# Layer 1's weights scaled in place with their low halves made by GpSimd, and four buffers for the first two units' probabilities

## The chip, the cores and the metric

The kernel runs on one core of a Trainium2 chip. The metric is the device time of one execution in microseconds (us); lower is better. TensorE (PE in the rows), VectorE (DVE), ScalarE (ACT), GpSimd (POOL) and the DMA queue of SyncE (SP, or SPq) work in parallel. Each runs its own list of instructions in order, and they wait for one another on semaphores only.

## The reference, cut to what matters

Two layers of masked attention over 128 graphs of 128 nodes, width 384, six heads of 64. Each layer is the same, with weights of its own:

```
h = max(layernorm(x), 0)                       # x: 128 x 128 x 384
q, k, v = h @ Wq + bq, h @ Wk + bk, h @ Wv + bv
probs = softmax(q k^T / 8 + (0 where adj else -9e15))
x = x + (probs @ v) @ Wf + bf
```

## The kernel before

A **unit** `t` is four graphs in one layer; there are 64 units (32 groups of graphs times two layers), and (t, i) is graph i of unit t. Units 0 to 3 belong to layer 0, unit 4 is the first one of layer 1, then the layers alternate. The work is a software pipeline written out by hand: a hand-written opening part, then `slot(t)` for t = 1 to 61, then a hand-written end (`last_units`). Every engine has a `slot(t)` of its own, and each goes through four quarters i = 0 to 3. In slot t TensorE forms the scores of unit t, the q, k and v projections of unit t + 1 (q and k in six chunks of 128 columns, two PSUM banks in turn), and the context products and output projections of graphs four to eight quarters back.

A float32 product is made as three float16 products of high and low halves (`three`, L665 to L667). So each weight needs a high half `w_hi` and a low half `w_lo`, both of the weight times a power of two, `w_scale`. Layer 0's are made in the opening part. Layer 1's are made in the quarters of slot 1, one weight per quarter in the order v, q, k, f: ScalarE writes `w_hi` (`weights_hi`, L915), VectorE writes `w_lo = w_raw * w_scale - w_hi` (`weights_lo`, L1207), each 128 x 1152. The first reader of layer 1's weights is the projection of unit 4, in slot 3.

The softmax chain of one graph: TensorE `score` (L779), VectorE `mask_and_min` (L1289), ScalarE `exp` (L986), VectorE `invert_sums`, GpSimd `scale_probs` (L540), VectorE `probs_turn` (L1230, a transpose in 32 x 32 blocks). Then SyncE's queue stores the blocks in DRAM (`keep_probs`, L360) and brings them back in turned order with four DMAs (`bring_probs`, L367), to `p_moved[i % 2]`. For units 0 and 1, TensorE multiplies `p_moved` with v in float32 (`apply_probs`, L759); from unit 2 on (`halved`), ScalarE casts the high half to `p_half` (`p_hi`, L961), GpSimd makes the low half (`p_lo`, L552), and the product has three float16 terms. h goes the same way over DRAM (`keep_h`, `bring_h`), and then `h_hi` (L940) and `h_lo` (L547) split it.

`p_half` is two tiles of 128 x 3 x 768 float16. Until unit 2 they hold no probabilities; layer 0's Wq and Wk are loaded into them at the start. There are two `p_moved` tiles, so the return of graph (t, i) waits until the graph two before it has been multiplied: `ctx_summed` counts the `apply_probs` done. For units 0 and 1 in the odd quarters SyncE's queue issues `bring_h` ahead of `bring_probs` (`late`).

Other names the steps touch: `ctx_hi` (L977) and `ctx_lo` (L1263) split a context product; `qk_hi_out` (L969) and `qk_lo_out` (L1269) take a chunk out of its PSUM bank, and the chunk two further on waits for that; `v_out` (L948) and `v_lo` (L1258) do so for v; `relu` (L926) waits for GpSimd's `norm` (L522 to L527), which waits for VectorE's `statistics`. TensorE's `project_v(t, i)` in the even quarters waits for `ctx_lo` of graph i of unit t - 2 (`ct_set`), `score(t, 0)` waits for the last `qk_lo_out` of unit t, and `apply_probs` of an odd graph i of unit t waits for `v_lo` of graph i of unit t + 2.

Of the kernel before, what the change touches and what calls it, by code (L numbers as in the profile page):

```python
# [21 lines left out]
def build(nc, x, adj, layers, out):  # L22
# [97 lines left out]
    with ExitStack() as ctx:  # L120
# [98 lines left out]
        scales_set = sem("scales_set")  # L219
        w_hi_set = sem("w_hi_set")  # L220
        weights_set = sem("weights_set")
        v_bias_spread = sem("v_bias_spread")
        out_bias_summed = sem("out_bias_summed")
# [82 lines left out]
        ps_value = small_bank(0)  # L306

        def moved_in_order(tile):

            return tile[:, :, :].rearrange("p a (c k) -> p c a k", c=KT)  # L310
# [10 lines left out]
        def _(sp):  # L321
# [41 lines left out]
            def bring_back(t, i, dram, moved, kept, back):  # L363

                wait(sp, kept[i], unit_count(t, 16, 16))
                for quad in range(QUADS):
                    sp.dma_start(moved[i % 2][quad * SQ:(quad + 1) * SQ, :, :],  # L367
                                 dram[i, :, :, quad, :].rearrange("a r n -> r a n")).then_inc(back[i], 16)
# [4 lines left out]
            def bring_probs(t, i):  # L373
                du, di = graph_at(t, i, -2)
                if halved(du):

                    sp.wait_ge(p_set, halved_count(du, di))
                else:
                    wait(sp, ctx_summed, unit_count(t, PER, i - 1))
                bring_back(t, i, p_dram, p_moved, p_kept, p_back)  # L380

# [4 lines left out]
            def bring_h(t, i):  # L386
                wait(sp, ht_set, unit_count(t - 1, PER, i - 1))
                bring_back(t - 1, i, h_dram, h_moved, h_kept, h_back)

# [6 lines left out]
            def slot(t):  # L396
                for i in range(PER):
                    pu, pi = graph_at(t, i, -2)
                    hu, hi = graph_at(t, i, 9)
                    su, si = graph_at(t, i, -6)  # L400
                    if exists(pu):
                        keep_probs(pu, pi)
                    if exists(hu):
                        keep_h(hu, hi)
                    if exists(su) and layer_of(su) == 1:
                        store(su, si)
                    if i == 0 and exists(t + 2):
                        load_adj(t + 2)
                    if exists(t + 4) and layer_of(t + 4) == 0:
                        load_x(t + 4, i)  # L410

                    late = i % 2 and pu < HALVED
                    if exists(pu) and not late:
                        bring_probs(pu, pi)
                    if exists(hu):
                        bring_h(hu, hi)
                    if exists(pu) and late:
                        bring_probs(pu, pi)

# [95 lines left out]
        def _(pool):  # L515
# [28 lines left out]
            def h_lo(t, i):  # L544
# [3 lines left out]
                                        in_order(ht_hi[b][:, :, rows]), ALU.subtract).then_inc(ht_set, 1)  # L548

            def p_lo(t, i):  # L550
                pool.wait_ge(p_hi_set, halved_count(t, i))
                nc.gpsimd.tensor_tensor(p_part(i, 1), p_moved[i % 2][:, :, :].rearrange("p a n -> p (a n)"), p_part(i, 0),  # L552
                                        ALU.subtract).then_inc(p_set, 1)

            def slot(t):
                for i in range(PER):
                    nu, ni = graph_at(t, i, 10)
                    hu, hi = graph_at(t, i, 8)
                    pu, pi = graph_at(t, i, -1)
# [12 lines left out]
            def last_units():
# [53 lines left out]
        def _(pe):  # L626
# [47 lines left out]
            def turn_first(i):  # L674
# [3 lines left out]
                mm.then_inc(first_turned, 1)  # L678

            def h_split(t, graphs):  # L680

# [5 lines left out]
            def project_v(t, i):  # L687
                b, l = unit_no(t) % 2, layer_of(t)
                h_split(t, i + 1)
                if unit_no(t) <= AHEAD and i == 0:  # L690
                    pe.wait_ge(weights_set, 4 * l + CAST_ORDER.index(2) + 1)
                cu, ci = graph_at(t, i, -8)
# [27 lines left out]
            def project_qk(t, piece):  # L720
# [4 lines left out]
                if c == 0 and chunk % KT == 0 and unit_no(t) <= AHEAD:  # L725
                    pe.wait_ge(weights_set, 4 * l + CAST_ORDER.index(chunk // KT) + 1)
                if c == 0:
# [8 lines left out]
            def apply_probs(t, i):  # L736
# [14 lines left out]
                else:  # L751
                    pe.wait_ge(p_back[i], unit_count(t, 16 * QUADS, 16 * QUADS))
                    terms = [(v_of(t, i), p_moved[i % 2][:, :, :].rearrange("p a n -> p (a n)"))]
                for c in range(PAIRS):
# [28 lines left out]
            def output(t, i):  # L783
# [6 lines left out]
                if unit_no(t) <= AHEAD and i == 0:  # L790
                    pe.wait_ge(weights_set, 4 * l + CAST_ORDER.index(3) + 1)
                for c in range(KT):
# [118 lines left out]
        def _(act):  # L911
            def weights_hi(l, j):

                act.wait_ge(w_scales_set, 3 if l else 1 if j == 2 else 2)
                nc.scalar.activation(w_hi[l][j][:, :, :], w_raw[l][j][:, :, :], ACT.Copy,  # L915
                                     scale=w_scale[l][:, j:j + 1]).then_inc(w_hi_set, 1)
# [38 lines left out]
            def p_hi(t, i):  # L955
                if (t, i) == (HALVED, 0):

                    act.wait_ge(weights_set, CAST_ORDER.index(1) + 1)
                act.wait_ge(p_back[i], unit_count(t, 16 * QUADS, 16 * QUADS))
# [161 lines left out]
        def _(dve):  # L1121
# [82 lines left out]

            def weights_lo(l, j):
                dve.wait_ge(w_hi_set, 4 * l + CAST_ORDER.index(j) + 1)
                nc.vector.scalar_tensor_tensor(out=w_lo[l][j][:, :, :], in0=w_raw[l][j][:, :, :],  # L1207
                                               scalar=w_scale[l][:, j:j + 1], in1=w_hi[l][j][:, :, :],
                                               op0=ALU.mult, op1=ALU.subtract).then_inc(weights_set, 1)
# [93 lines left out]
            def slot(t):  # L1303
                for i in range(PER):
# [25 lines left out]
                    if exists(t):  # L1330
                        mask_and_min(t, i)
                    if t == 1:
                        weights_lo(1, CAST_ORDER[i])
                    if exists(t + 1):
# [79 lines left out]
            first_lo(1)  # L1414
            weights_lo(0, 2)
            find_largest_bias(0)
# [12 lines left out]
            spread_v_bias(0)  # L1429
            weights_lo(0, 0)  # L1430
            h_turn(1, 2)
            statistics(1, 3)
            statistics(2, 0)
            weights_lo(0, 1)
            statistics(2, 1)
# [3 lines left out]
            qk_lo_out(0, 1)  # L1439
            weights_lo(0, 3)  # L1440
            qk_lo_out(0, 2)
# [62 lines left out]
```

## Time and profile before

| | |
|---|---|
| median of 3 runs | 1856.35 us (1855.97 to 1858.41) |
| the profiled execution, its own time | 1854.17 us |
| its span in the trace | 1852.4 us |
| busy: TensorE, VectorE, ScalarE, GpSimd | 1822.2, 1630.8, 1556.1, 1485.9 us |

The span is the time from the first to the last instruction of the profiled execution, and its own time is 1.8 us more. The profiled execution is 2.2 us below the median of the runs. "Busy" is time in which an engine executes instructions; the granted clock (PEclk) is that of TensorE, 1.00 at 2.4 GHz and 0.50 at 1.2 GHz. Times in the rows are us from the start of the span.

### The profile page before, as it was taken

The numbers are of one execution on the slowest core, as the hardware profiler recorded it, in microseconds if no ns is written. First come the engines' busy times: TensorE is split into PE (matmuls) and PEld (weight loads), VectorE is DVE, ScalarE is ACT, GpSimd is POOL, SyncE is SP. The second block draws the span as 40 slices with busy tenths as digits, with TensorE's granted clock in tenths as the row PEclk, the third lists the DMA queues.
The fourth block names the chain that finished last, engine by engine and source line by source line (L and its number), as shares of the span: only waits on it lengthen the run. The fifth ranks groups of instructions, "written<-read, shape, count | busy, mean of one in ns | idle before, by whom it ended". The sixth has DMA issues, their size and how long they took to land.

```text
span 1852.4 us, 54319 instructions
## 1 busy us (share of the span) xinstructions
PE 1822.2 (98%) x17210; PEld 1050.3 (57%) x17210; DVE 1630.8 (88%) x5555; ACT 1556.1 (84%) x4789; POOL 1485.9 (80%) x1777
## 2 busy tenths in 40 slices
PE   7899999999999999999999999999999999999998
PEld 3455555555555555555555555555555555555555
DVE  7988888899898898988989889888898988889876
ACT  5768888888888888888888888888888888888884
POOL 4668888888888888888888888888888888888772
PEclk8999999999999999999999999999999999999999
DMA  6646766667666666666666666666666666666655
GB/s 193 171 144 198 211 193 196 195 200 212 198 206 189 197 209 203 205 196 194 202 208 204 198 196 201 194 209 205 191 198 197 209 204 200 201 185 189 186 178 182
DMA packets 439943, 363.32 MB, mean 196 GB/s; under 512 B 207701, under 2 KB 406889, under 8 KB 439657
## 3 DMA queue, kind: packets, MB, share of 16 engines
q1 hardware_dynamic: 439656, 359.86, 65.3%
q8 instruction: 137, 2.24, 0.5%
q14 instruction: 150, 1.22, 0.2%
HBM read 184.30 MB, written 175.37 MB: 194 GB/s over the span
## 4 chain that ended last, share of the span: by engine, by line
PE 86%; DVE 4%; DMA 4%; SPq 3%; issue 2%; POOL 1%; ACT 1%; DVEq 0%; POOLq 0%; ACTq 0%
PE ps_qk L665 12%; PE ps_shared L665 12%; PE ps_shared L667 12%; PE ps_shared L666 12%; PE ps_qk L667 12%; PE ps_qk L666 12%; PE ps_shared L759 7%; PE ps_scores L779 7%; SPq L367 3%; DMA p_dram<-p_blocks 2%; DVE probs L1289 1%; DVE p_blocks L1230 1%; DVE qk_lo L1269 1%; POOL probs L540 1%; DMA p_half<-in_L_gnn_Wk 0%
## 5 line engine op out<-in xcount | busy, mean ns | idle before, releaser
L986 ACT ACTIVATE probs<-probs,row_min 128x128 f32<-128x128 f32 x1512 | 583.0, 390 | 2.5 <-DVE row_rcp L1254 1.5
L540 POOL TENSOR_TENSOR probs<-probs,row_rcp 128x768 f32<-128x768 f32 x252 | 371.4, 1474 | 214.1 <-DVE row_rcp L1254 213.9
L1289 DVE CUSTOM_DVE_ANT_0 probs<-ps_scores,mask,minus_scale 128x128 f32<-128x128 f32 x1512 | 429.5, 347 | 0.9 <-issue 0.6
L552 POOL TENSOR_TENSOR p_half<-p_moved,p_half 128x768 f16<-128x768 f32 x236 | 388.0, 1644 | 3.2 <-ACT p_half L961 3.2
L1269 DVE SCALAR_TENSOR_TENSOR qk_lo<-ps_qk,qk_bias,qk_hi 128x512 f16<-128x512 f32 x384 | 277.7, 747 | 60.1 <-ACT qk_hi L969 59.2
L986 ACT ACTIVATION_READ_ACCUMULATOR probs<-probs,row_min 128x1 f32 x1512 | 288.0, 191 | 0.0
L969 ACT ACTIVATE qk_hi<-ps_qk,qk_bias 128x512 f16<-128x512 f32 x384 | 258.3, 673 | 15.1 <-PE ps_qk L667 15.1
L1300 DVE SCALAR_TENSOR_TENSOR x_tile<-ps_shared,out_scale,x_tile 128x384 f32<-128x384 f32 x256 | 157.6, 616 | 123.5 <-PE ps_shared L667 122.1
L536 POOL TENSOR_TENSOR x_tile<-x_tile,out_bias 128x384 f32<-128x384 f32 x256 | 257.8, 1008 | 1.1 <-DVE out_bias L1213 1.1
L665 PE MATMUL ps_shared<-wf_hi,ct_hi 128*128 128x384 f16 x768 | 250.7, 326 | 2.4 <-DVE ct_lo L1263 2.4
L666 PE MATMUL ps_shared<-wf_lo,ct_hi 128*128 128x384 f16 x768 | 250.7, 326 | 0.0
L667 PE MATMUL ps_shared<-wf_hi,ct_lo 128*128 128x384 f16 x768 | 250.6, 326 | 0.0
L665 PE MATMUL ps_shared<-wv_hi,ht_hi 128*128 128x384 f16 x756 | 247.6, 327 | 0.0
L666 PE MATMUL ps_shared<-wv_lo,ht_hi 128*128 128x384 f16 x756 | 247.4, 327 | 0.0
L667 PE MATMUL ps_shared<-wv_hi,ht_lo 128*128 128x384 f16 x756 | 247.4, 327 | 0.0
L1230 DVE STREAM_TRANSPOSE p_blocks<-probs 128x768 f32<-128x768 f32 x252 | 244.0, 968 | 3.7 <-POOL probs L540 3.7
L547 POOL TENSOR_TENSOR ht_lo<-h_moved,ht_hi 128x384 f16<-128x384 f32 x252 | 234.1, 929 | 8.0 <-ACT ht_hi L940 8.0
L948 ACT ACTIVATE v<-ps_shared 128x384 f16<-128x384 f32 x236 | 115.7, 490 | 143.5 <-PE ps_shared L667 142.7
L665 PE MATMUL ps_qk<-ht_hi,wq_hi 128*128 128x512 f16 x576 | 219.7, 381 | 2.1 <-DVE qk_lo L1269 1.8
L665 PE MATMUL ps_qk<-ht_hi,wk_hi 128*128 128x512 f16 x576 | 219.3, 381 | 0.0
L666 PE MATMUL ps_qk<-ht_lo,wq_hi 128*128 128x512 f16 x576 | 218.8, 380 | 0.0
L667 PE MATMUL ps_qk<-ht_hi,wq_lo 128*128 128x512 f16 x576 | 218.8, 380 | 0.0
(144 smaller groups left out, 3973.2 us busy)
## 6 DMA issues: line engine op xcount, KB each, us to landing
p_dram<-p_blocks SPq DMA_DIRECT2D x256, 384.0 KB, 2.4
p_moved<-p_dram SPq DMA_DIRECT2D x1024, 96.0 KB, 2.3
h_dram<-h_blocks SPq DMA_DIRECT2D x252, 192.0 KB, 2.6
h_moved<-h_dram SPq DMA_DIRECT2D x1008, 48.0 KB, 2.0
x_tile<-in_x SPq DMA_DIRECT2D x128, 192.0 KB, 2.9
out_x<-x_tile SPq DMA_DIRECT2D x128, 192.0 KB, 2.7
adj_u<-in_adj SPq DMA_DIRECT2D x64, 64.0 KB, 2.5
wv_raw<-in_L_gnn_Wv SPq DMA_DIRECT2D x2, 576.0 KB, 5.0
```

The lines of the kernel that those rows point to most:

```text
L536: nc.gpsimd.tensor_tensor(xs, xs, out_bias[l][:, :], ALU.add).then_inc(res_ready, 1)
L540: nc.gpsimd.tensor_tensor(probs_of(t, i), probs_of(t, i), row_rcp[i % 2][:, :].rearrange("p (a o) -> p a o", o=1) .to_broadcast([P, HEADS, ...
L547: nc.gpsimd.tensor_tensor(in_order(ht_lo[b][:, :, rows]), moved_in_order(h_moved[i % 2]), in_order(ht_hi[b][:, :, rows]), ALU.subtract).th ...
L552: nc.gpsimd.tensor_tensor(p_part(i, 1), p_moved[i % 2][:, :, :].rearrange("p a n -> p (a n)"), p_part(i, 0), ALU.subtract).then_inc(p_set, 1)
L665: pe.matmul(acc, a_hi, b_hi, start=first, stop=False)
L666: pe.matmul(acc, a_hi, b_lo, start=False, stop=False)
L667: return pe.matmul(acc, a_lo, b_hi, start=False, stop=last)
L969: nc.scalar.activation(qk_hi[b][:, chunk, :], ps_qk[chunk % QK_BANKS][:, :], ACT.Identity, bias=qk_bias[layer_of(t)][:, chunk // KT, chunk ...
L986: ins = nc.scalar.activation(tile[:, s, :], tile[:, s, :], ACT.Exp, bias=row_min[i % 2][:, s:s + 1], scale=-1.0, accum_out=row_sum[i % 2][ ...
L1230: return nc.vector.transpose(out.rearrange("p b (c k) -> p b c k", c=cols), view.rearrange("p (c b r) -> p b c r", c=cols, b=QUADS))
L1269: nc.vector.scalar_tensor_tensor(out=qk_lo[b][:, chunk, :], in0=ps_qk[chunk % QK_BANKS][:, :], scalar=qk_bias[layer_of(t)][:, chunk // KT, ...
L1289: ins = nc.vector.tensor_tensor_reduce(tile[:, s, :], score_bank(i, s // PAIRS)[:, (s % PAIRS) * P:(s % PAIRS + 1) * P], mask[b][:, i, :], ...
```

## The change

Two edits. First, layer 1's weights in slot 1: ScalarE multiplies the raw float32 weight by its scale in place, waits for that (`weights_scaled`), and casts the result to `w_hi`; GpSimd, as the last step of the quarter, subtracts `w_hi` from the scaled weight (`next_weights_lo`). VectorE has no part in it any more, and TensorE waits on `next_weights_set` for layer 1. Second, the probabilities of graphs 2 and 3 of units 0 and 1 come back into the `p_half` tiles, seen as float32, so four buffers are in turn. The wait of a return is for the graph four before it instead of two, up to the first two graphs of unit 2; and `bring_probs` stands ahead of `bring_h` in every quarter.

```
         def p_back_tile(t, i):
+            if t < HALVED and i >= 2:
+                return p_half[i % 2][:, 0:2, :].rearrange("p a n -> p (a n)").bitcast(F32).rearrange("p (a n) -> p a n", a=QUADS)
+            return p_moved[i % 2][:, :, :]
...
             def bring_probs(t, i):
                 du, di = graph_at(t, i, -2)
+                eu, ei = graph_at(t, i, -4)
                 if halved(du):
                     sp.wait_ge(p_set, halved_count(du, di))
-                else:
-                    wait(sp, ctx_summed, unit_count(t, PER, i - 1))
-                bring_back(t, i, p_dram, p_moved, p_kept, p_back)
+                elif t >= A - 1:
+                    sp.wait_ge(ctx_summed, unit_count(t, PER, i - 1))
+                elif exists(eu):
+                    sp.wait_ge(ctx_summed, unit_count(eu, PER, ei + 1))
+                elif i >= 2:
+                    sp.wait_ge(weights_set, CAST_ORDER.index(1) + 1)
+                bring_back(t, i, p_dram, p_back_tile(t, i), p_kept, p_back)
...
-                    late = i % 2 and pu < HALVED
-                    if exists(pu) and not late:
+                    if exists(pu):
                         bring_probs(pu, pi)
                     if exists(hu):
                         bring_h(hu, hi)
-                    if exists(pu) and late:
-                        bring_probs(pu, pi)
...
+            def next_weights_lo(j):
+                pool.wait_ge(w_hi_set, 4 + CAST_ORDER.index(j) + 1)
+                nc.gpsimd.tensor_tensor(w_lo[1][j][:, :, :], w_raw[1][j][:, :, :], w_hi[1][j][:, :, :], ALU.subtract
+                                        ).then_inc(next_weights_set, 1)
...
                     if exists(hu):
                         h_lo(hu, hi)
+                    if t == 1:
+                        next_weights_lo(CAST_ORDER[i])
...
-                    terms = [(v_of(t, i), p_moved[i % 2][:, :, :].rearrange("p a n -> p (a n)"))]
+                    terms = [(v_of(t, i), p_back_tile(t, i).rearrange("p a n -> p (a n)"))]
...
             def weights_hi(l, j):
                 act.wait_ge(w_scales_set, 3 if l else 1 if j == 2 else 2)
+                if l == 1:
+                    if j == 3:
+                        act.wait_ge(out_bias_summed, LAYERS)
+                    nc.scalar.activation(w_raw[1][j][:, :, :], w_raw[1][j][:, :, :], ACT.Copy,
+                                         scale=w_scale[1][:, j:j + 1]).then_inc(weights_scaled, 1)
+                    act.wait_ge(weights_scaled, CAST_ORDER.index(j) + 1)
+                    nc.scalar.activation(w_hi[1][j][:, :, :], w_raw[1][j][:, :, :], ACT.Copy).then_inc(w_hi_set, 1)
+                    return
...
             def p_hi(t, i):
-                if (t, i) == (HALVED, 0):
-                    act.wait_ge(weights_set, CAST_ORDER.index(1) + 1)
...
-                    if t == 1:
-                        weights_lo(1, CAST_ORDER[i])
```

ScalarE's list in slot 1, quarter 2, before (the softmax's exp of graph (1, 1), the high half of Wk, the high halves of the context products (0, 1) and (0, 2), and the relu of unit 4):

```order
L986 ACTIVATE probs1,row_sum1<-probs1,row_min1 128x128 x5
L915 ACTIVATE wk_hi1<-wk_raw1,w_scale1 128x1152 [waits w_scales_set]
L977 ACTIVATE ct_hi1<-ps_shared1 128x384 [waits ctx_summed]
L977 ACTIVATE ct_hi0<-ps_shared0 128x384 [waits ctx_summed,out_summed]
L926 ACTIVATE h0<-x_tile0,shift0,rstd0 128x384 [waits norm_ready,h_blocked]
```

The same place after the change:

```order
L1013 ACTIVATE probs1,row_sum1<-probs1,row_min1 128x128 x5
L940 ACTIVATE wk_raw1<-wk_raw1,w_scale1 128x1152 [waits w_scales_set]
L943 ACTIVATE wk_hi1<-wk_raw1 128x1152 [waits weights_scaled]
L1004 ACTIVATE ct_hi1<-ps_shared1 128x384 [waits ctx_summed]
L1004 ACTIVATE ct_hi0<-ps_shared0 128x384 [waits ctx_summed,out_summed]
L956 ACTIVATE h0<-x_tile0,shift0,rstd0 128x384 [waits norm_ready,h_blocked]
```

One instruction of 128 x 1152 stands ahead of the context casts that was not there; each quarter of slot 1 has one like it.

GpSimd's list at the end of quarter 1 of slot 1 and the start of quarter 2, after the change (before, the L563 row is not there; h's low half is followed at once by the norm of unit 4):

```order
L551 TENSOR_TENSOR probs0<-probs0,row_rcp0 128x768 [waits rcp_ready]
L558 TENSOR_TENSOR ht_lo1<-h_moved1,ht_hi1 128x3x128 [waits ht_hi_set]
L563 TENSOR_TENSOR wq_lo1<-wq_raw1,wq_hi1 128x1152 [waits w_hi_set]
L533 TENSOR_SCALAR var_eps0<-mean_var0 128x1 [waits mean_found,h_ready]
```

The product of the weight's low half moved from VectorE's list to the place between `h_lo` and the next `norm`.

SyncE's queue in slot 1, quarter 1, before (the return of graph (0, 3) is last):

```order
L360 DMA p_dram<-p_blocks1 128x768 [waits p_blocked]
L360 DMA h_dram<-h_blocks0 128x384 [waits h_blocked,h_back2]
L331 DMA x_tile4<-in_x 128x384
L367 DMA h_moved0<-h_dram 32x4x96 [waits h_kept2,ht_set]
L367 DMA h_moved0<-h_dram 32x4x96 x3
L367 DMA p_moved1<-p_dram 32x4x192 [waits p_kept3,ctx_summed]
L367 DMA p_moved1<-p_dram 32x4x192 x3
```

and after:

```order
L368 DMA p_dram<-p_blocks1 128x768 [waits p_blocked]
L368 DMA h_dram<-h_blocks0 128x384 [waits h_blocked,h_back2]
L339 DMA x_tile4<-in_x 128x384
L375 DMA p_half1<-p_dram 32x4x192 [waits p_kept3,weights_set]
L375 DMA p_half1<-p_dram 32x4x192 x3
L375 DMA h_moved0<-h_dram 32x4x96 [waits h_kept2,ht_set]
L375 DMA h_moved0<-h_dram 32x4x96 x3
```

The return goes to `p_half1`, stands ahead of h's, and waits for layer 0's weights in place of a context product. The return of (2, 1), in slot 2, quarter 3, reads the same in both lists; its wait on `ctx_summed` is for 6 products (through graph (1, 1)) where it was for 8 (through graph (1, 3)).

## Rows read from the trace of the kernel before

**Rows 1.** The page, part 1 (busy) and TensorE's granted clock of part 2.

```profile
PE 1822.2 (98%) x17210; PEld 1050.3 (57%) x17210; DVE 1630.8 (88%) x5555; ACT 1556.1 (84%) x4789; POOL 1485.9 (80%) x1777
...
PEclk8999999999999999999999999999999999999999
```

**Rows 2.** Windows: from:to, length, busy time of PE, PEld, DVE, ACT, POOL, clock.

```profile
75.00:102.30 27.30, 23.83 (x175) 12.92 (x173) 27.23 (x79) 22.62 (x68) 19.47 (x22) 0.99 0.61 176
102.30:106.40 4.10, 4.10 (x61) 3.73 (x62) 3.13 (x8) 1.41 (x7) 1.64 (x4) 0.62 0.08 17
...
134.00:152.00 18.00, 15.59 (x165) 9.15 (x162) 12.94 (x45) 12.39 (x41) 12.45 (x16) 1.00 0.67 184
...
165.00:1000.00 835.00, 834.78 (x8029) 483.19 (x8024) 746.66 (x2560) 725.97 (x2232) 704.87 (x835) 1.00 0.67 200
```

**Rows 3.** Timeline of TensorE: start, length, what, [idle before, releaser].

```profile
86.31 1.53 PE L759 MATMUL ps_shared<-p_moved,v 128*64 128x128 f32 x24 [0.62 <-DVE v L1258]
90.37 0.33 PE L665 MATMUL ps_shared<-wv_hi,ht_hi 128*128 128x384 f16 x1
102.30 0.29 PE L779 MATMUL ps_scores<-qk_hi 64*128 64x128 f16 x2 [2.67 <-DVE qk_lo L1269]
143.18 0.39 PE L665 MATMUL ps_qk<-ht_hi,wq_hi 128*128 128x512 f16 x1 [1.23 <-DVE qk_lo L1269]
150.51 1.22 PE L759 MATMUL ps_shared<-p_half,v 128*64 128x128 f16 x36 [1.18 <-DVE v L1258]
```

**Rows 4.** The chain that ended last, slot 2: start, length, what.

```profile
102.30 2.10 PE ps_scores L779 x36
104.40 1.98 PE ps_shared L759 x24
...
118.16 1.11 PE ps_scores L779 x36
119.27 1.46 PE ps_shared L759 x24
```

**Rows 5.** VectorE: window of L1207 alone, then a row of its timeline.

```profile
75.00:102.30 27.30, 8.35 (x4) 0.99 0.61 176
...
100.84 1.40 DVE L1269 SCALAR_TENSOR_TENSOR qk_lo<-ps_qk,qk_bias,qk_hi 128x512 f16<-128x512 f32 x2
```

**Rows 6.** Timeline of ScalarE.

```profile
72.21 1.25 ACT L915 ACTIVATE wv_hi<-wv_raw,w_scale 128x1152 f16<-128x1152 f32 x1
84.10 0.47 ACT L948 ACTIVATE v<-ps_shared 128x384 f16<-128x384 f32 x1
87.93 0.85 ACT L977 ACTIVATE ct_hi<-ps_shared 128x384 f16<-128x384 f32 x2
99.87 0.66 ACT L969 ACTIVATE qk_hi<-ps_qk,qk_bias 128x512 f16<-128x512 f32 x1
139.40 0.84 ACT L961 ACTIVATE p_half<-p_moved 128x768 f16<-128x768 f32 x1 [3.77 <-DMA p_moved<-p_dram]
```

**Rows 7.** Timeline of GpSimd.

```profile
77.55 2.04 POOL L547 TENSOR_TENSOR ht_lo<-h_moved,ht_hi 128x384 f16<-128x384 f32 x1
102.21 0.91 POOL L547 TENSOR_TENSOR ht_lo<-h_moved,ht_hi 128x384 f16<-128x384 f32 x1
130.28 1.65 POOL L552 TENSOR_TENSOR p_half<-p_moved,p_half 128x768 f16<-128x768 f32 x1
```

**Rows 8.** SyncE's queue: waits from 70 to 165 (total, times, longest), then its timeline.

```profile
SPq L367 <- PE ps_shared L759: 9.1, 4, 4.1
...
129.10 0.34 SPq L360 DMA_DIRECT2D p_dram<-p_blocks  x1
134.58 2.84 SPq L367 DMA_DIRECT2D p_moved<-p_dram  x4
```

**Rows 9.** The page, part 6: DMA issues, KB each, median us from issue to landing.

```profile
p_dram<-p_blocks SPq DMA_DIRECT2D x256, 384.0 KB, 2.4
p_moved<-p_dram SPq DMA_DIRECT2D x1024, 96.0 KB, 2.3
```

More of the change, by code:

```diff
@@ L220, in build @@
         w_hi_set = sem("w_hi_set")
+        weights_scaled = sem("weights_scaled")
         weights_set = sem("weights_set")
+        next_weights_set = sem("next_weights_set")
         v_bias_spread = sem("v_bias_spread")
@@ L306, in build, with p_back_tile @@
         ps_value = small_bank(0)
+        def p_back_tile(t, i):
+            if t < HALVED and i >= 2:
+                return p_half[i % 2][:, 0:2, :].rearrange("p a n -> p (a n)").bitcast(F32).rearrange("p (a n) -> p a n", a=QUADS)
+            return p_moved[i % 2][:, :, :]
         def moved_in_order(tile):
@@ L366, in bring_back @@
                 for quad in range(QUADS):
-                    sp.dma_start(moved[i % 2][quad * SQ:(quad + 1) * SQ, :, :],
+                    sp.dma_start(moved[quad * SQ:(quad + 1) * SQ, :, :],
                                  dram[i, :, :, quad, :].rearrange("a r n -> r a n")).then_inc(back[i], 16)
@@ L387, in bring_h @@
                 wait(sp, ht_set, unit_count(t - 1, PER, i - 1))
-                bring_back(t - 1, i, h_dram, h_moved, h_kept, h_back)
+                bring_back(t - 1, i, h_dram, h_moved[i % 2], h_kept, h_back)
             def store(t, i):
@@ L678, in turn_first, with weights_split @@
                 mm.then_inc(first_turned, 1)
+            def weights_split(l, j):
+                pe.wait_ge((weights_set, next_weights_set)[l], CAST_ORDER.index(j) + 1)
             def h_split(t, graphs):
@@ L690, in project_v @@
                 if unit_no(t) <= AHEAD and i == 0:
-                    pe.wait_ge(weights_set, 4 * l + CAST_ORDER.index(2) + 1)
+                    weights_split(l, 2)
                 cu, ci = graph_at(t, i, -8)
@@ L725, in project_qk @@
                 if c == 0 and chunk % KT == 0 and unit_no(t) <= AHEAD:
-                    pe.wait_ge(weights_set, 4 * l + CAST_ORDER.index(chunk // KT) + 1)
+                    weights_split(l, chunk // KT)
                 if c == 0:
@@ L790, in output @@
                 if unit_no(t) <= AHEAD and i == 0:
-                    pe.wait_ge(weights_set, 4 * l + CAST_ORDER.index(3) + 1)
+                    weights_split(l, 3)
                 for c in range(KT):
@@ L1203, in find_other_scales, with weights_lo @@
                 ins.then_inc(scales_set, 1)
[L1205 to L1208, printed above, removed]
+            def weights_lo(j):
+                dve.wait_ge(w_hi_set, CAST_ORDER.index(j) + 1)
+                nc.vector.scalar_tensor_tensor(out=w_lo[0][j][:, :, :], in0=w_raw[0][j][:, :, :],
+                                               scalar=w_scale[0][:, j:j + 1], in1=w_hi[0][j][:, :, :],
                                                op0=ALU.mult, op1=ALU.subtract).then_inc(weights_set, 1)
@@ L1414, in _ @@
             first_lo(1)
-            weights_lo(0, 2)
+            weights_lo(2)
             find_largest_bias(0)
@@ L1429, in _ @@
             spread_v_bias(0)
-            weights_lo(0, 0)
+            weights_lo(0)
             h_turn(1, 2)
@@ L1433, in _ @@
             statistics(2, 0)
-            weights_lo(0, 1)
+            weights_lo(1)
             statistics(2, 1)
@@ L1439, in _ @@
             qk_lo_out(0, 1)
-            weights_lo(0, 3)
+            weights_lo(3)
             qk_lo_out(0, 2)
```

## The prediction

> **What bounds the kernel now.** I read the page first: TensorE is busy 98% of the span, and its granted clock is at or near the upper level in all but the first slice [rows 1]. Then the windows: from 165 us on TensorE is busy 834.78 of 835 us [rows 2], so nothing that the change does can shorten that part; a gain or loss has to come from the opening, and it then stays as a plain shift to the end. In slot 1 (75 to 102.3) it is another picture: VectorE is busy 27.23 of 27.30 us, TensorE 23.83, ScalarE 22.62, GpSimd 19.47 [rows 2]. VectorE is the bound of that stretch. TensorE's timeline says where it shows: 0.62 us of waiting for `v_lo` at 86.31, and 2.67 us at 102.30, where `score(2, 0)` needs the last `qk_lo_out` of unit 2 [rows 3], the pair that VectorE starts at 100.84 [rows 5]. Behind the long wait the clock is at its lower level: 0.62 is the mean from 102.3 to 106.4 [rows 2], and the same two groups of matmuls take 2.10 and 1.98 us there, but 1.11 and 1.46 us two quarters later [rows 4]. After that TensorE runs without a gap until slot 3, where it is busy 15.59 of 18.00 us [rows 2], with waits of 1.23 and 1.18 us [rows 3]. Their cause is read on ScalarE: `p_hi(2, 1)` starts at 139.40 after 3.77 us idle for the DMA that brings the probabilities back [rows 6]. SyncE's queue stored that graph at 129.10, but issued the return only at 134.58, as `ctx_summed` had to reach graph (1, 3) [rows 8]. Four returns of this stretch wait for a context product, 9.1 us in all [rows 8].
>
> **What the change takes away.** *VectorE:* four instructions of L1207, 8.35 us in slot 1 [rows 5]. It falls from 27.2 to 18.9 of 27.3 us and is no bound any more. *The return of (2, 1):* stored at 129.10, landed 2.4 us later [rows 8, 9], so issued from 131.6 in place of 134.58, 3.0 us earlier at an unchanged pace. The store itself comes earlier too, since the queue is not held by the waits of (0, 3), (1, 1) and (1, 3) before it. With its 2.84 us of issues and 2.3 us to landing [rows 8, 9] it has landed at 136.7 at the latest instead of about 139.4. The DMA of h behind it and the store and return of (2, 2) move by as much. Of the 3.77 us at most 1.1 stay. TensorE's two waits of 1.23 and 1.18 us hang on this chain (late `p_hi`, then `qk_hi_out` behind it, then the next `p_hi`), each shorter than the 2.7 us won, so I take both as gone: 2.4 us. The transfers are the same in number and size; (0, 3), (1, 1) and (1, 2) come earlier than anyone needs them, at no gain of their own.
>
> **What it adds.** *ScalarE:* in each quarter of slot 1 one instruction of 128 x 1152 more. The `w_hi` instruction takes 1.25 us [rows 6]; the scaling differs only in its output type, so I take 1.25 for it, the short wait between the two included, as the plain cast after it should be a little cheaper than the scaled one. Bounds: 0.84 us, the cast of 128 x 768 [rows 6], and 1.4, where the wait comes on top. *GpSimd:* 128 x 384 takes 0.91 us, 128 x 768 takes 1.65 [rows 7], so 0.74 us for 384 more, and 128 x 1152 some 2.4 us; four are 9.6 us. The bound above is a product stretched by VectorE: `h_lo` took 2.04 us instead of 0.91 [rows 7] just while VectorE ran L1207, a factor of 2.24. But that is the instruction which goes away, and such stretching goes with it. GpSimd goes from 19.5 to about 29 us less what stretching had cost, 1.1 us at each of at least two products: about as full as the quarter can bear. *The order on ScalarE* is the real price, because its new instruction stands ahead of casts that TensorE waits for.
>
> Here the Trainium skill (GPSIMD Engine Reference, When to use GPSIMD) speaks against the edit: elementwise work with two inputs belongs on VectorE, GpSimd being about half as fast. The rows bear that out only weakly: 8.35 us on VectorE against an estimated 9.6 on GpSimd. The same page's Specifications name VectorE instructions with two SBUF inputs as those that contend with GpSimd, and the 2.04 against 0.91 us agree.
>
> **Slot 1 followed through.** Quarter 0: ScalarE had waited for GpSimd's norm anyway, so the pace is unchanged, and TensorE's path does not move. Quarter 1: exp is released as before, then ScalarE's list is 1.25 us later. `v_out(2, 1)`, at 84.10 [rows 6], comes at 85.35 and ends at 85.8; `v_lo(2, 1)` follows once VectorE has done the `qk_lo_out` ahead of it, and TensorE starts `apply_probs(0, 1)` at about 86.8 instead of 86.31 [rows 3]: 0.5 us lost although VectorE is free. Quarter 2: the second added instruction puts the two `ctx_hi` (87.93, 0.85 long [rows 6]) 2.5 us later, ending at 91.3; half a us of `ctx_lo` behind them, and `project_v(2, 2)`, which started at 90.37 [rows 3], starts at 91.9: TensorE, ready at 90.85, waits 1.1 us and is now 1.5 behind. From there VectorE's release pays. Before, 90.37 to 102.30 took 11.93 us, of them 2.67 waiting [rows 3], so 9.26 of work; TensorE is through at 91.9 + 9.26 = 101.2. The last `qk_hi_out` was at 99.87 and took 0.66 [rows 6]. ScalarE had idled for GpSimd's norm ahead of it, so only about 0.35 us of the added time is left: it ends at 100.9, and one `qk_lo_out` of 0.7 us (half of 1.40 [rows 5]) ends at 101.7, since no `weights_lo` stands ahead of it. `score(2, 0)` starts at about 101.8 instead of 102.30: **0.5 us** won, after a wait of 0.6 us where there were 2.67.
>
> The clock then should not fall: waits of 1.23 and 1.18 us in slot 3 left it at 1.00 [rows 2, 3], and the new ones are 1.4 (0.6 before, 0.5 of delay, 0.3 for which TensorE is ready earlier), 1.1 and 0.6. So the two groups cost 1.11 + 1.46 instead of 2.10 + 1.98 [rows 4]: **1.5 us**.
>
> **The sum**: 0.5 + 1.5 + 2.4 = 4.4 us. The profiled execution's own time goes from 1854.17 to 1849.8 us; the median of the runs shown stands 2.2 us above it, so I say 1856.35 - 4.4 = **1851.9 us**. Bounds of the terms: slot 1 from -1 (ScalarE at 1.4 and the full delay) to +3.3 (0.62 and 2.67 both gone), clock 0 to 1.5, slot 3 from 1.2 to 2.4; together 0.2 to 7.2 us.
>
> **The rivals.** A change under 0.2% (3.7 us) can hardly be told from none with this kernel.
> (a) *The clock falls all the same*, behind the waits of 1.4 and 1.1 us that lie 4 us apart. For it: no row shows two so near. Against: the pair in slot 3 is just as long and held. Then a stretch like that from 102.3 to 106.4 is only moved: 2.9 us gain, 1853.4.
> (b) *Slot 3's wait is hidden anyway or has another cause next in line*: one of the two waits stays, 1.2 us. Then 3.2 us, 1853.1.
> (c) *More is won*: the added ScalarE work is absorbed by its idle time (27.3 - 22.6 = 4.7 us in slot 1 [rows 2], nearly the 5.0 added), so that the waits of slot 1 vanish: 1849.1.
> (d) *ScalarE takes VectorE's place*: this one ends on the other side. If none of the 5.0 us is absorbed, the last `qk_hi_out` starts at 104.9, `score(2, 0)` at 106.3: 4.0 us lost, the clock falls as before, and only slot 3's 2.4 come back: 1858. It decides once less than 1.6 us of the added 5.0 are absorbed (then slot 1 loses more than slot 3's 2.4). Against it: ScalarE's 4.7 us of idle time; for it: that idle time is waiting for norms, which are themselves queued behind GpSimd's new product.
> (e) *GpSimd becomes the bound*: if the products take 2.24 x 2.4 = 5.4 us, three of them stand ahead of the `h_lo` of 102.21 [rows 7], 16 us against some 8 idle (27.3 - 19.5) and 2 given back. It ends 6 us later at 109.1, and TensorE, which needs it for unit 3's first chunk at 104.4 in my forecast, gets it 2.7 us behind the old 106.4, less 2.4 in slot 3: no change, 1856.7. Against it: what stretched GpSimd's rows was L1207, and that is gone. It is what the Trainium skill's page named above would lead one to expect (GPSIMD Engine Reference).
>
> **How the numbers follow.** Forecast 0.46, (a) 0.16, (b) 0.13, (c) 0.10, (d) 0.08, (e) 0.07. The forecast is over 3.7 us in some four of five of its shades, (c) always, (a) and (b) seldom: faster 0.51. (d) and (e) are within 0.2% as worked out; they and unknown effects of the new queue order pass 3.7 us of loss only with something on top: slower 0.07. Same 0.42. The range reaches from (c) to short of (d): 1849.0 to 1857.2.
>
> **What would show it.** VectorE without L1207 rows in slot 1 and with gaps; ScalarE with four more 1.25-us rows; four GpSimd rows near 2.4 us, and `h_lo` at 0.91 throughout. TensorE: a wait near 91 for `ctx_lo`, under 1 us at the start of slot 2, clock 1.00 behind it, no waits in slot 3; `p_hi(2, 1)` without its 3.77 us. Wrong if the scaling takes much over 1.3 us, if the clock falls anywhere from 86 to 106, or if TensorE still waits from 134 to 152.

## The result, and the profile after

The changed kernel takes 1851.31 us (median of 9 runs, 1849.64 to 1853.11), beside 1856.35 us for the kernel before in the same measurement (9 runs, 1852.76 to 1858.96). The ratio is 0.9972, 95% interval 0.9963 to 0.9981: a gain of 3.5 to 6.9 us; the medians lie 5.0 apart. In a later measurement the ratio was 0.9977 (0.9967 to 0.9988). The forecast was 1851.9 us. For the profiled execution 1849.8 us was forecast; it took 1853.11, and a second one 1851.50.

The page of the kernel after, part 1 and TensorE's clock [rows 1]:

```profile
PE 1821.8 (98%) x17210; PEld 1050.4 (57%) x17210; DVE 1621.9 (88%) x5551; ACT 1561.2 (84%) x4793; POOL 1490.9 (81%) x1781
...
PEclk8999999999999999999999999999999999999999
```

VectorE has 8.9 us less to do, ScalarE and GpSimd 5 us more each. (GpSimd's four new products are 9.5 us; four of its other rows, stretched before, give 4.0 back.) TensorE's work is what it was. The windows of [rows 2], in the kernel after (length; PE, PEld, DVE, ACT, POOL busy; clock):

```profile
75.00:102.30 27.30, 24.27 (x199) 13.59 (x199) 21.30 (x77) 25.78 (x70) 23.51 (x25) 1.00 0.65 187
102.30:106.40 4.10, 4.10 (x51) 2.60 (x46) 4.07 (x15) 2.54 (x9) 3.32 (x5) 1.00 0.52 162
...
134.00:152.00 18.00, 18.00 (x159) 10.34 (x158) 15.82 (x58) 15.11 (x46) 15.45 (x19) 1.00 0.67 192
```

In slot 1 VectorE fell from 27.23 to 21.30 us and ScalarE rose from 22.62 to 25.78: ScalarE is the fullest engine there now. The clock from 102.3 on is 1.00 instead of 0.62, and slot 3 has no gap left. TensorE's rows behind a wait in slots 1 to 3, where [rows 3] had four:

```profile
86.37 0.88 PE L780 MATMUL ps_shared<-p_moved,v 128*64 128x128 f32 x12 [1.36 <-DVE v L1285]
91.67 0.32 PE L683 MATMUL ps_shared<-wv_hi,ht_hi 128*128 128x384 f16 x1 [1.07 <-DVE ct_lo L1290]
101.53 0.23 PE L800 MATMUL ps_scores<-qk_hi 64*128 64x128 f16 x2 [0.61 <-DVE qk_lo L1296]
```

The first is `apply_probs(0, 1)`, the second `project_v(2, 2)`, the third `score(2, 0)`.

**A finer measure than the time.** The nine runs of one kernel differ by 3 to 6 us, more than the terms of the sum. Every trace has TensorE's scores, though, and the distance from the first matmul of `score(1, 0)` to that of a later score measures the opening alone. Behind `score(4, 0)`, half a slot takes 14.02 us in both kernels, so `score(4, 0)` closes the account. Each row below is read from TensorE's timeline, start minus start, in us; the early clock is that of the window 70 to 76 us (more on it below):

| kernel | (1, 2) | (2, 0) | (2, 2) | (3, 0) | (3, 2) | (4, 0) | gain at (4, 0) | early clock |
|---|---|---|---|---|---|---|---|---|
| before | 15.10 | 32.89 | 48.68 | 63.14 | 78.75 | 94.04 | | 0.72 |
| after | 14.81 | 32.51 | 46.86 | 61.22 | 75.42 | 89.44 | 4.60 | 0.72 |
| after, second profile | 14.86 | 32.54 | 46.90 | 61.25 | 75.46 | 89.48 | 4.56 | 0.72 |
| weights alone | 14.08 | 31.77 | 46.13 | 61.95 | 77.29 | 92.87 | 1.17 | 1.00 |
| buffers alone | 15.10 | 32.88 | 48.80 | 63.15 | 77.35 | 91.38 | 2.66 | 1.00 |
| before, filler in the wait | 15.08 | 32.88 | 47.23 | 62.77 | 78.13 | 93.42 | 0.62 | 0.72 |
| after, old wait of (2, 0), (2, 1) | 14.09 | 31.78 | 46.14 | 60.49 | 75.46 | 90.99 | 3.05 | 1.00 |
| after, subtraction on VectorE | 15.10 | 33.77 | 49.51 | 63.87 | 78.07 | 92.09 | 1.95 | 1.00 |
| weights in slot 2 | 14.76 | 29.64 | 44.58 | 61.60 | 75.80 | 89.83 | 4.21 | 0.72 |
| weights ahead of relu | 13.94 | 31.26 | 45.61 | 59.97 | 74.17 | 88.19 | 5.85 | 1.00 |
| weights in even quarters | 14.58 | 30.30 | 44.66 | 59.43 | 73.63 | 87.65 | 6.39 | 0.72 |
| the same, second profile | 16.07 | 31.69 | 46.05 | 60.82 | 75.02 | 89.04 | 5.00 | 0.54 |
| the same, early filler | 13.93 | 30.28 | 44.63 | 59.40 | 73.61 | 87.63 | 6.41 | 1.00 |

The kernel after gains 0.38 us up to `score(2, 0)`, 1.44 to `score(2, 2)`, 0.10 to `score(3, 0)` and 2.68 in slot 3.

### The profile page after: what moved, and what is told of

Its sections match the earlier page's. It is cut to its first block, busy times and chain, and to the rows that moved or that the text cites. A ratio compares the mean times of both kernels' runs of the same rounds, so it can differ in the third digit from the quotient of the medians.

```text
span 1851.3 us, 54324 instructions
## 1 busy us (share of the span) xinstructions
PE 1821.8 (98%) x17210; PEld 1050.4 (57%) x17210; DVE 1621.9 (88%) x5551; ACT 1561.2 (84%) x4793; POOL 1490.9 (81%) x1781
## 4 chain that ended last, share of the span: by engine, by line
PE 86%; DVE 4%; DMA 3%; SPq 3%; issue 2%; ACT 1%; POOL 1%; DVEq 0%; ACTq 0%; POOLq 0%
PE ps_qk L683 12%; PE ps_shared L683 12%; PE ps_shared L685 12%; PE ps_shared L684 12%; PE ps_qk L684 12%; PE ps_qk L685 12%; PE ps_shared L780 7%; PE ps_scores L800 7%; SPq L375 2%; DMA p_dram<-p_blocks 1%; DVE probs L1316 1%; DMA p_moved<-p_dram 1%; DVE qk_lo L1296 1%; POOL probs L551 1%; ACT probs L1013 1%
## 5 line engine op out<-in xcount | busy, mean ns | idle before, releaser
L988 ACT ACTIVATE p_half<-p_moved 128x768 f16<-128x768 f32 x236 | 197.4, 836 | 25.5 <-DMA p_moved<-p_dram 24.5
```

## The experiments

**The weights edit alone.** The kernel after with `p_back_tile` always `p_moved`, the old waits of `bring_probs` and the old order:

```
-                return p_half[i % 2][:, 0:2, :] ...
...
+                else:
+                    wait(sp, ctx_summed, unit_count(t, PER, i - 1))
...
+                    late = i % 2 and pu < HALVED
```

> The weights edit without the four buffers. Measured on TensorE's timeline from the start of score(1, 0): before, score(2, 0) starts 32.89 us later, score(2, 2) 48.68 and score(4, 0) 94.04. My theory (the two edits act at different places and add): score(2, 0) 0.4 us earlier than before, score(2, 2) 1.8 to 1.9 earlier (the clock stays up), and the waits of 1.2 and 1.2 us in slot 3 stay, so score(4, 0) is 1.9 us earlier; the time falls by about 2 us. Rival (slot 3's waits come from VectorE's lateness in slot 1 and not from the return of (2, 1)): score(4, 0) 4.6 us earlier, as with both edits.

Measured: 1853.42 us, ratio 0.9993 (0.9983 to 1.0003), not to be told from before. In the trace `score(2, 2)` is 2.55 us ahead of before; 0.7 of it is an early clock that held in this execution, which leaves the 1.8 expected. But at `score(3, 0)` only 1.19 is left, and 1.17 at `score(4, 0)`. I had expected slot 3's waits to stay, and they did; that slot 2 would give back 1.36 us I had not. TensorE, ScalarE and SyncE's queue in slot 2 of this kernel:

```profile
117.35 1.53 PE L777 MATMUL ps_shared<-p_moved,v 128*64 128x128 f32 x24 [0.81 <-DVE v L1285]
131.18 0.23 PE L797 MATMUL ps_scores<-qk_hi 64*128 64x128 f16 x2 [0.51 <-DVE qk_lo L1296]
```

```profile
114.95 0.53 ACT L967 ACTIVATE ht_hi<-h_moved 128x384 f16<-128x384 f32 x1 [1.19 <-DMA h_moved<-h_dram]
127.33 0.84 ACT L988 ACTIVATE p_half<-p_moved 128x768 f16<-128x768 f32 x1 [1.40 <-issue]
```

```profile
104.86 0.38 SPq L368 DMA_DIRECT2D p_dram<-p_blocks  x1
...
109.81 1.74 SPq L375 DMA_DIRECT2D p_moved<-p_dram  x4
...
118.38 1.80 SPq L375 DMA_DIRECT2D p_moved<-p_dram  x4
120.28 0.38 SPq L368 DMA_DIRECT2D p_dram<-p_blocks  x1
...
123.06 2.48 SPq L375 DMA_DIRECT2D p_moved<-p_dram  x4
```

Rows of the queue in before, at the same places:

```profile
108.69 0.38 SPq L360 DMA_DIRECT2D p_dram<-p_blocks  x1
...
111.38 1.74 SPq L367 DMA_DIRECT2D p_moved<-p_dram  x4
...
120.12 1.73 SPq L367 DMA_DIRECT2D p_moved<-p_dram  x4
```

At the store of graph (1, 2), 104.86, the queue is 3.65 us ahead of before, counted from `score(1, 0)`. But the return of that graph is issued only 4.95 us after the store, as the store lands late; in before it was 2.69, so 1.39 us of the lead are left. All that stands behind it in the queue is then late: h's return (the 1.19 us on ScalarE, and with `v_out` behind it the 0.81 us on TensorE), and the return of (1, 3), at 118.38. The blocks of (2, 0) were ready at 118.71, but their store goes at 120.28 and their return at 123.06; `p_hi(2, 0)` starts after 1.40 us idle, and the `qk_hi_out` behind it makes `score(3, 0)` wait 0.51. In the kernel after, the return of (2, 0) is at 120.40, and `p_hi(2, 0)` starts without a wait. How much slot 2 would give back had that store landed sooner, this one profile doesn't show.

**The buffers alone.** The kernel after with layer 1's `w_lo` back on VectorE, as `weights_lo(1, CAST_ORDER[i])` behind `mask_and_min`, and no scaling in place:

```
-                        next_weights_lo(CAST_ORDER[i])
...
+                    if t == 1:
+                        weights_lo(CAST_ORDER[i], 1)
```

> The four buffers, their waits and the queue order, without the weights edit. My theory: score(2, 0) and score(2, 2) start as before (32.89 and 48.68 us after score(1, 0)), the clock falls behind the 2.67-us wait as before, slot 3 has no waits for qk_lo or v, and score(4, 0) is 2.4 to 2.7 us earlier than before's 94.04; the time falls by about 2.5 us. Rival (one wait stays, with another cause next in line): 1.2 us earlier. Rival (the buffers only help once slot 1 is shorter): no change.

Measured: 1853.19 us, ratio 0.9990 (0.9980 to 0.9999). The trace is as expected: `score(2, 0)` moves by 0.01 us (`score(2, 2)` comes 0.12 later), the clock falls behind the 2.7-us wait, and slot 3 wins 2.67 us (0.01 behind before at `score(3, 0)`, 2.66 ahead at `score(4, 0)`). Clock of the window behind that wait:

```profile
102.70:107.00 4.30, 4.30 (x61) 0.60 0.39 142
```

**The clock by itself.** The kernel before, with idle matmuls in the long wait:

```
                 if (t, i) == (2, 0):
                     pe.wait_ge(masked, unit_count(t, PER, i - 1))
                     for _ in range(10):
                         pe.matmul(ps_scores[0][:, :], idle_work[:, 0:P], idle_work[:, :], start=True, stop=True)
```

> The kernel before, with ten idle matmuls of 128 x 512 on TensorE, written to a bank that score(2, 0) overwrites, ahead of the wait for the last qk_lo of unit 2. They take about 2.2 us of a wait of 2.67 and change no other work. If the clock falls because TensorE idled there: score(2, 0) starts as before (32.89), the clock is 1.00 from 102 to 107, and score(2, 2) comes 1.4 to 1.5 us earlier than 48.68; the time falls by 1.5 us. If the clock falls for another reason, or the lower clock costs nothing: score(2, 2) as before or up to 0.3 later, the time unchanged.

TensorE's row of the filler, and the window behind it:

```profile
99.32 2.32 PE L769 MATMUL ps_scores<-idle_work 128*128 128x512 f16 x10
```

```profile
102.30:106.40 4.10, 4.10 (x68) 1.00 0.15 39
```

`score(2, 0)` starts as before (32.88), the clock stays at 1.00, and `score(2, 2)` comes 1.45 us earlier: the term is shown by itself, in one profile. But at `score(3, 0)` 0.37 is left of it: `p_hi(2, 0)` starts after 2.01 us idle. The queue had come 1.45 us earlier too, up to the return of (1, 3); the four issues of this one then took 3.12 us, where before took 1.73 for the same, and the store of (2, 0) behind them was back at the old place. The time, 1853.39 us, ratio 0.9996 (0.9986 to 1.0005), does not show a gain; in the opening, 0.62 us is left of the 1.5 that I expected.

```profile
118.55 3.12 SPq L367 DMA_DIRECT2D p_moved<-p_dram  x4
121.77 0.38 SPq L360 DMA_DIRECT2D p_dram<-p_blocks  x1
...
128.22 0.84 ACT L965 ACTIVATE p_half<-p_moved 128x768 f16<-128x768 f32 x1 [2.01 <-issue]
```

**The old wait for (2, 0) and (2, 1).** The kernel after with one condition changed:

```
-                elif t >= A - 1:
+                elif t >= A - 1 or t == HALVED:
```

> The kernel after, with the returns of (2, 0) to (2, 1) waiting for the context product two graphs before, as in the kernel before. If that one wait of (2, 1) is slot 3's cause: the slot-3 waits come back (about 1.2 and 1.2 us), score(3, 0) is as in the kernel after (1.9 us earlier than before), score(4, 0) is 1.9 earlier instead of 4.6. If the order of the queue and the earlier returns of units 0 and 1 do it: score(4, 0) 4.6 earlier as in the kernel after.

Measured: 1851.66 us, ratio 0.9980 (0.9970 to 0.9989). Up to `score(3, 0)` it gains 2.65 us (1.92 and the 0.7 of the early clock); in slot 3 it gains 0.40, where the kernel after gains 2.68. ScalarE's and SyncE's rows of slot 3, and TensorE's:

```profile
134.99 0.84 ACT L988 ACTIVATE p_half<-p_moved 128x768 f16<-128x768 f32 x1 [2.49 <-DMA p_moved<-p_dram]
```

```profile
124.47 0.34 SPq L368 DMA_DIRECT2D p_dram<-p_blocks  x1
...
131.45 1.75 SPq L375 DMA_DIRECT2D p_moved<-p_dram  x4
```

```profile
139.42 0.39 PE L683 MATMUL ps_qk<-ht_hi,wq_hi 128*128 128x512 f16 x1 [0.59 <-DVE qk_lo L1296]
...
146.98 1.22 PE L780 MATMUL ps_shared<-p_half,v 128*64 128x128 f16 x36 [1.42 <-DVE v L1285]
```

Graph (2, 1) is stored at 124.47 and returned at 131.45, as [rows 8] show it for the kernel before. In the kernel after the return follows once the store has landed:

```profile
125.25 0.34 SPq L368 DMA_DIRECT2D p_dram<-p_blocks  x1
125.90 0.34 SPq L368 DMA_DIRECT2D h_dram<-h_blocks  x1
128.19 1.75 SPq L375 DMA_DIRECT2D p_moved<-p_dram  x4
```

So the two old waits cost 2.3 of slot 3's 2.7 us; ScalarE waits for no probabilities at (2, 0), so it is the wait of (2, 1).

**The subtraction on VectorE.** The kernel after with `next_weights_lo` on VectorE, where `weights_lo` had stood:

```
-                nc.gpsimd.tensor_tensor(w_lo[1][j] ..., w_raw[1][j] ..., w_hi[1][j] ..., ALU.subtract
+                nc.vector.tensor_tensor(w_lo[1][j] ..., w_raw[1][j] ..., w_hi[1][j] ..., ALU.subtract
```

> The kernel after, with the subtraction on VectorE (where weights_lo stood) from the scaled weight, and none on GpSimd. It tells what GpSimd's part is worth, and what stretched its rows. If VectorE instructions with two SBUF inputs stretch GpSimd's: h_lo takes 2.0 us instead of 0.91 beside them, and the four take 6.5 to 10 us. TensorE: VectorE is full again and ScalarE has the added work, score(2, 0) 0.5 to 2.5 us later than before's 32.89, the clock falls behind a long wait. If ScalarE's place in the list is the only bound: score(2, 0) at 32.5 as in the kernel after.

Measured: 1852.78 us, ratio 0.9984 (0.9974 to 0.9993); `score(2, 0)` 0.88 us later than before, after a wait of 2.6, and the clock at 0.63 over the 4.1 us behind it. VectorE's and GpSimd's rows at one place, and GpSimd's in the kernel after:

```profile
77.85 1.66 DVE L1238 TENSOR_TENSOR wv_lo<-wv_raw,wv_hi 128x1152 f16<-128x1152 f32 x1
```

```profile
78.25 2.03 POOL L558 TENSOR_TENSOR ht_lo<-h_moved,ht_hi 128x384 f16<-128x384 f32 x1
```

```profile
77.17 0.91 POOL L558 TENSOR_TENSOR ht_lo<-h_moved,ht_hi 128x384 f16<-128x384 f32 x1
78.04 2.37 POOL L563 TENSOR_TENSOR wv_lo<-wv_raw,wv_hi 128x1152 f16<-128x1152 f32 x1
```

VectorE's plain subtraction of two SBUF inputs, without a scale operand, stretches the `h_lo` that starts behind it from 0.91 to 2.03 us. The Trainium skill (GPSIMD Engine Reference, Specifications) names VectorE instructions with two SBUF inputs as those that contend with GpSimd, and the traces agree. Not every row beside one is stretched: at 93.17 `h_lo` started 0.24 us ahead of VectorE's and took 0.92 us, and VectorE's took 1.90, where 1.60 is its shortest. It is shown too that ScalarE's added work loses in slot 1 when VectorE is hardly relieved (its four take 7.03 us instead of 8.35).

**The weights in slot 2.** `if t == 2` in place of `if t == 1`, on ScalarE and GpSimd.

> The kernel after, with the weights' scaling, cast and GpSimd product in the four quarters of slot 2 instead of slot 1. In slot 1 neither VectorE nor ScalarE has them. From the start of score(1, 0): before, score(2, 0) is at 32.89 us and score(4, 0) at 94.04; after, 32.51 and 89.44. If slot 1's three new waits (1.36, 1.07, 0.61) are the price of the place in ScalarE's list: score(2, 0) at about 29.5, and slot 2 pays part of it back (ScalarE has 5.2 us idle there), score(4, 0) at 86.5 to 89.0. If something else bounds slot 1 once VectorE is free: score(2, 0) near 32.5. If the cost only moves to slot 2: score(4, 0) at 89.4 or later.

Measured: 1849.51 us, ratio 0.9960 (0.9945 to 0.9975). Slot 1 is 3.25 us shorter than before, as both the old waits (0.62 and 2.67) and most of the new ones are gone. As it is rid of all the work on three engines, this doesn't tell whether the new waits were the price of ScalarE's place or of the work itself. Slot 2 pays: from `score(2, 2)` to `score(3, 0)` it takes 17.02 us against 14.36 in the kernel after, with two waits:

```profile
120.16 0.32 PE L683 MATMUL ps_shared<-wv_hi,ht_hi 128*128 128x384 f16 x1 [1.07 <-DVE ct_lo L1290]
130.74 0.23 PE L800 MATMUL ps_scores<-qk_hi 64*128 64x128 f16 x2 [1.34 <-DVE qk_lo L1296]
```

At `score(4, 0)` it is 0.4 us behind the kernel after, so the lower time (4 runs) is not backed by the opening. From there to the end its profile takes 1688.5 us, those of the kernel after 1692.8 and 1690.1, and that of before 1689.0.

**The weights ahead of relu.** Later in the same quarter of slot 1, behind `ctx_hi` and the first `qk_hi_out`:

```
-                    if t == 1:
-                        weights_hi(1, CAST_ORDER[i])
                     for cu, ci in pair_at(t, i):
...
+                    if t == 1:
+                        weights_hi(1, CAST_ORDER[i])
                     if exists(nu):
                         relu(nu, ni)
```

> The kernel after, with the two ScalarE instructions of a weight later in each quarter of slot 1: behind the context casts and the first qk_hi, ahead of relu, where ScalarE waited for GpSimd's norm. If the order on ScalarE is what makes TensorE wait at 91.7 (1.07 us, for ctx_lo): that wait vanishes, the one for v_lo in quarter 1 (1.36) stays, and score(2, 0) is 0.5 to 1.2 us earlier than in the kernel after. If the sum of ScalarE's work bounds slot 1: score(2, 0) within 0.3 us of 32.51.

Measured: 1849.03 us, ratio 0.9952 (0.9936 to 0.9969). The 1.07-us wait is gone and `score(2, 0)` is 1.25 us earlier than in the kernel after, 0.7 of it the early clock; the rest, some 0.5, is the low end of what I expected. This is the test of the place alone: the same work in the same quarters, later in the list. Part of the removed wait came back as a longer one at `score(2, 0)`:

```profile
86.63 0.88 PE L780 MATMUL ps_shared<-p_moved,v 128*64 128x128 f32 x12 [1.35 <-DVE v L1285]
...
101.42 0.23 PE L800 MATMUL ps_scores<-qk_hi 64*128 64x128 f16 x2 [1.47 <-DVE qk_lo L1296]
```

**The weights in the even quarters of slots 1 and 2**, ahead of relu, and GpSimd's products likewise:

```
+                    if t in (1, 2) and i % 2 == 0:
+                        weights_hi(1, CAST_ORDER[2 * (t - 1) + i // 2])
                     if exists(nu):
                         relu(nu, ni)
```

> The kernel after, with the four weights in quarters 0 and 2 of slots 1 and 2, ahead of relu. ScalarE idles there for the norm, and the odd quarters (where v_lo of the odd graph was late) are free of them. If ScalarE's idle time is what can be had: no wait in slot 1, score(2, 0) at 29.5 to 30, small waits in slot 2, score(4, 0) at 86.0 to 87.5, and the time 5 to 8 us below before. If GpSimd's product bounds: a wait for ht_lo or norm shows, score(4, 0) above 88.

Measured: 1849.22 us, ratio 0.9956 (0.9941 to 0.9971). `score(4, 0)` is 6.39 us ahead of before, 1.8 ahead of the kernel after at the same early clock. The waits for v and `ctx_lo` in slot 1 are gone; 1.21 us at `score(2, 0)` and 0.34 at `score(3, 0)` are left.

**Three once more, side by side**: the kernel after, the even quarters, and these with a filler of nine idle matmuls ahead of `score(1, 0)`.

> The kernel after once more, beside the next two kernels. In the traces so far the clock fell behind the wait of 2.4 us ahead of score(1, 0) in some executions and not in others, with the same wait, and where it held, score(1, 2) came 0.7 us earlier (14.1 us after score(1, 0) instead of 14.8). If that is chance of the execution: score(1, 2) at 14.8 or 14.1, and everything behind it as in the first trace apart from that, score(2, 2) to score(4, 0) taking 42.6 us. Time 0.2 to 0.3% below before.

> The kernel with the weights in quarters 0 and 2 of slots 1 and 2 once more, for its time beside that of the kernel after. By its first trace it is 1.8 us ahead of the kernel after at score(4, 0), so 0.1% faster: about 0.35 to 0.4% below before. If 1.8 us in the opening are not seen in the time: the same ratio as the kernel after within 0.03%.

> The same, with nine idle matmuls of 128 x 512 (1.9 us) on TensorE in the wait of 2.4 us ahead of score(1, 0), to a bank that score(1, 0) overwrites. If the wait is what lets the clock fall: clock 1.00 from 70 to 76 us in every execution, score(1, 2) 14.0 to 14.1 us after score(1, 0), score(4, 0) 7.1 us earlier than before instead of 6.4. If the fall has another cause: clock about 0.7 there, score(1, 2) at 14.6.

Measured: 1851.50 us, ratio 0.9977 (0.9967 to 0.9988); 1848.77, 0.9958 (0.9945 to 0.9972); 1847.99, 0.9959 (0.9947 to 0.9972). TensorE's windows 66 to 70 and 70 to 76 in the second and the third (length, busy, clock):

```profile
66.00:70.00 4.00, 1.63 (x32) 1.00 0.88 243
70.00:76.00 6.00, 5.12 (x38) 0.54 0.72 190
```

```profile
66.00:70.00 4.00, 3.57 (x28) 1.00 0.89 265
70.00:76.00 6.00, 4.44 (x59) 1.00 0.66 188
```

With the filler the clock held. `score(1, 2)` comes 0.65 us earlier than in the first profile of the even quarters, but `score(4, 0)` only 0.02: TensorE then waits 0.6 us for v in slot 1. One profile does not show that the filler held the clock: it held in five kernels without one (last section). Against my 7.1, the opening gains 6.41, and the time is that of the kernel without the filler. The even quarters have now twice had a ratio below that of the kernel after, by 0.0016 and 0.0019, more than the 0.001 that the opening explains; the intervals overlap.

## Why the prediction was right

**Slot 1, 0.5 us: 0.38.** The walk through the quarters held nearly row for row. From `score(1, 0)`, `apply_probs(0, 1)` starts 0.45 us later than before (0.5 forecast) and `project_v(2, 2)` 1.69 later (1.5). Only `score(1, 2)`, 0.29 us earlier, was not in it: quarter 0 was taken as unchanged. The scaling takes 1.24 to 1.25 us, the cast behind it 1.16, GpSimd's product 2.37 to 2.38 (2.4 forecast). The waits forecast as 1.4, 1.1 and 0.6 are 1.36, 1.07 and 0.61. Most of VectorE's 8.35 us is not seen on TensorE, since ScalarE's 5 us stand ahead of the casts TensorE needs. The place alone was some 0.5 us of that price, as the weights ahead of relu show. The even quarters win 1.8 more than the kernel after, but they change the place and take half of the work out of slot 1, so it stays open how much of it is the place.

**The clock, 1.5 us: 1.44**, and 1.45 by itself with the filler. Rival (a) fell: the two waits 4 us apart left it at 1.00, in both profiles of the kernel.

**Slot 3, 2.4 us: 2.68**, of it 2.3 by the wait of (2, 1), as the old wait alone shows. The two waits of before are 2.41 us; where the other 0.27 come from was not followed up. Rival (b) fell.

**The sum, 4.4 us: 4.60** in the opening, 5.0 in the medians. That the rest of the span is a plain shift held for the kernel, not for each execution: from `score(4, 0)` to the end before's profile takes 1689.0 us and the two of the kernel after 1692.8 and 1690.1, so the forecast of 1849.8 us for the profiled execution missed.

**A step that stays open:** "(0, 3), (1, 1) and (1, 2) come earlier than anyone needs them, at no gain of their own". I also took the terms as a sum of two independent edits. Apart, the two gained 1.17 us (0.7 of an early clock in it) and 2.66 us in the opening, together 4.60. Without the buffers slot 2 gave back 1.36 us of the weights edit and 1.08 us of the filler's gain; in the six profiles with the buffers and no weights in slot 2 it gave back nothing (with the old wait for (2, 0) and (2, 1): 2.54 ahead at `score(2, 2)`, 2.65 at `score(3, 0)`).

But each loss is one profile, and each began at one slow step of SyncE's queue: a store that was 4.95 us ahead of its return, and issues of 3.12 us. Such steps are not rare. Between 165 and 1700 us of before, one in ten returns follows its store by over 3.6 us (median 2.5), and one in ten takes over 2.7 us to issue (median 1.75). What differs is what they cost: with the buffers, the stores of (1, 2) and (2, 0) were 3.95 and 3.34 us ahead of their returns in the second profile of the kernel after, 3.84 and 3.23 in the buffers alone, and TensorE waited nowhere in slot 2. So the earlier returns do leave the queue more room there. Whether slot 2 gives anything back without them when no step is slow is not shown, and the ratios of the times (0.9993, 0.9990, together 0.9972 and 0.9977) are too close to tell. If it does, my sum came out right by luck, as it counted slot 1 and the clock in full.

**(c), (d), (e):** ScalarE's idle time did not absorb the work (c), but slot 1 didn't lose either (d); `score(2, 0)` behind before's is seen only where VectorE keeps the subtraction. GpSimd did not become the bound (e): its products took 2.37 to 2.38 us and not 5.4, every `h_lo` in slot 1 took 0.91 to 0.92, and so the stretching that (e) needs went with VectorE's instruction.

## What to carry to other kernels

Work moved to an engine with idle time is priced by what stands behind it in that engine's list too: the same instructions later in the same quarters gave some 0.5 us more, and spread over twice as many quarters, where the engine waited anyway, 1.8 more. A queue whose waits cost nothing now may have no room left once the stretch before is shorter, so look at its room at the new pace. Where terms are smaller than the spread of the times, measure between two marks of the trace on the bound engine.

## What was not expected of the hardware

The same wait of 2.4 us ahead of `score(1, 0)`, with TensorE busy 1.62 to 1.79 of 4.00 us from 66 to 70, was followed by a lower clock in some executions and not in others: 0.72 in the window 70 to 76 in before, before with the filler at its later place, after (twice), the weights in slot 2 and the even quarters, 0.54 in the second profile of the even quarters, and 1.00 with the weights alone, the buffers alone, the old wait, the subtraction on VectorE and the weights ahead of relu. Between the kernel after and that with the weights alone it makes 0.7 us at `score(1, 2)`. Where VectorE bounds the stretch it makes nothing: before (0.72) and the buffers alone (1.00) both have `score(1, 2)` at 15.10, the latter with a wait of 0.99 us for `qk_lo` at 79.93 where before has 0.17. What decides the clock there is open. The wait of 2.6 to 2.7 us ahead of `score(2, 0)` was followed by the lower clock in all three kernels that had it (before 0.62, the buffers alone 0.60, the subtraction on VectorE 0.63; one profile each).

The profiled execution of the kernel after is only 1.1 us below that of before. In it ScalarE waited 44.8 us for DMAs between 165 and 1700 us, beside 19.7 in before and 14.7 in the second profile of the same kernel. Waits of ScalarE and TensorE in that stretch (total, times, longest), before, after, and after the second time:

```profile
ACT p_half L961 <- DMA p_moved<-p_dram: 9.9, 23, 1.1
ACT ht_hi L940 <- DMA h_moved<-h_dram: 9.8, 21, 0.9
PE ps_scores L779 <- DVE qk_lo L1269: 1.2, 2, 1.0
```

```profile
ACT p_half L988 <- DMA p_moved<-p_dram: 23.2, 39, 1.7
ACT ht_hi L970 <- DMA h_moved<-h_dram: 21.6, 32, 1.6
PE ps_scores L800 <- DVE qk_lo L1296: 3.1, 5, 1.2
```

```profile
ACT ht_hi L970 <- DMA h_moved<-h_dram: 10.0, 16, 1.2
ACT p_half L988 <- DMA p_moved<-p_dram: 4.7, 10, 0.8
PE ps_scores L800 <- DVE qk_lo L1296: 0.3, 1, 0.3
```

TensorE's waits there are 0.3 to 3.1 us and go with ScalarE's, with the execution and not with the kernel. That late returns cause them is not followed row by row. The 1.9 us between before and the kernel after are half of the 3.9 us by which the latter's first profile is longer behind `score(4, 0)`.
